# One kernel of a graph transformer: each layer gets its own numbers of sorted blocks

## The chip, the cores and the metric

The kernel runs on one core of one Trainium2 chip. The time is the device time of one execution in microseconds (us); lower is better. Engine names are those of the profile: PE (matmuls, PEld its weight loads), DVE (vector), ACT (scalar), POOL (GpSimd), SP (SyncE, which issues DMAs here).

## The reference

x is 6250 nodes x 128, and there are 200000 edges (src, dst), sorted by dst, plus one loop per node. Two layers are applied, then x + layers(x) is normalized.

```python
for l in range(2):
    xn = layernorm(x); pos = xn @ Wpos + bpos + deg_z * Wdeg + bdeg; xp = xn + pos
    q, k, v = xp @ Wq + bq, xp @ Wk + bk, xp @ Wv + bv        # 8 heads of 16
    att = clip(sum_d(q[dst] * k[src]) / 4, -50, 50)
    alpha = softmax of att over the edges of one dst
    x = x + segment_sum(v[src] * alpha, dst) @ Wo + bo
    x = x + gelu(layernorm(x) @ W1 + b1) @ W2 + b2            # 512 wide
out = layernorm(x_in + x)
```

## The kernel before

**Tables.** The nodes form NT = 49 tiles of 128. Each layer reads its keys and values from a table in HBM (kv_table[l], 256 floats a node) and its queries from q_table[l]. Set-up computes layer 0's tables; the node steps of layer 0 write layer 1's.

**Two kinds of edge units.** Since the edges are sorted by target, a tile of targets owns about 4096 of them. The first JB = 49 - 8 = 41 tiles are done *by chunks*: 1024 edges each (T = 8 tiles of 128), CPT = 4 chunks per tile of targets, CA = 4 x 41 + 1 = 165 chunks a layer. GpSimd fetches the 1024 key and value rows with eight indirect DMAs (`gather`, L1900 to L1910) into a ring of RING_KV = 4 buffers (three in kv_ring, the fourth in arena); it waits until the messages of the chunk four before are made (msg_ready). The last NB = 8 tiles are done *by blocks*: their edges have been sorted by source tile once, in layer 0, so that each source tile has 128 slots. A block part handles seven source tiles: SyncE loads their rows whole (source_rows, 896 KB, `load_sources`), and PE picks the row of each edge by a product with a one-hot matrix (`gather_rows`, L897); no indirect DMA. OB = 7 parts make a tile, UB = 56 a layer.

**A unit's work.** Both kinds go through the same steps: PE spreads the queries over the edges (L938 for chunks, L971 for blocks), DVE multiplies with the keys (L1603), reduces and clips (L1612 to L1618), ACT takes exp (L1201), DVE makes the messages (L1627, one per unit), PE sums them (L954, L987), DVE adds the sums to the accumulators (L1653, L1659, L1665). All of this is issued in an order worked out when the program is built: `unit_order` spreads the block parts evenly over the chunks from chunk FIRST_B = 17 on, the order is the same in both layers (NU = 221 units), and every unit has two slots. Into the slots go the node steps (`node_starts`, `node_steps`: 33 steps for a tile in layer 0, 27 in layer 1; projection, feed-forward, norms) and, in layer 0 only, the sorts.

**The sorts.** `sort_steps` gives each of the eight tiles 23 steps, beginning eight slots before the first part of the tile before it. A sort loads ST = 40 tiles of edges from start_tile, makes one-hots and ranks on DVE and PE (L1002, L1008, L1015), and writes the result to sorted_table, from which both layers read (`load_block`). The PSUM banks of sorts, node steps and edge sums come from one ring (`node_banks`).

**Set-up.** `count_cells` counts, for the edges from chunk COUNT_C = 163 on, how many fall into each (target tile, source tile) cell: one-hots on DVE (L1346, COUNT_STEPS = 9 steps of 32 columns, the last of 8), products on PE (L784). It shares the loop with the degree histogram (L1332, L1335, L775). `plan_chunks` checks that the graph is regular (chunk 163 starts below node 41 x 128, no cell over 128, starts at most 40 tiles apart, ...); if not, a general path runs instead.

**Places.** Semaphore targets are counted through both layers as l * NU + u (units), l * CA + c (chunks), l * UB + b (parts).

Of the kernel before, what the change touches and what calls it, by code (L numbers as in the profile page):

```python
# [72 lines left out]
NB = 8  # L73
JB = NT - NB
CA = CPT * JB + LAG
# [3 lines left out]
UB = NB * OB  # L79

FIRST_B = 17
# [19 lines left out]
def unit_order():  # L101

    order, b = [], 0
    for c in range(CA):
        order.append(("chunk", c))
        if b < UB and (c + 1 - FIRST_B) * UB >= b * (CA - 1 - FIRST_B):
            order.append(("block", b))
            b += 1
    assert b == UB
    return order  # L110


UNITS = unit_order()
NU = len(UNITS)
CHUNK_AT = [u for u, (what, _) in enumerate(UNITS) if what == "chunk"]
BLOCK_AT = [u for u, (what, _) in enumerate(UNITS) if what == "block"]
assert all(b - a > 2 for a, b in zip(BLOCK_AT, BLOCK_AT[1:]))


def is_block(u):  # L120
    return 0 <= u < NU and UNITS[u][0] == "block"


def tiles_of(u):

    return TB if is_block(u) else T


def parts_of(u):

    return 2 if is_block(u) else 1


def last_unit(j):

    return CHUNK_AT[min(CPT * (j + 1), CA - 1)] if j < JB else BLOCK_AT[(j - JB) * OB + OB - 1]

TILES = sorted(range(NT), key=lambda j: (last_unit(j), j))  # L140
POS = [TILES.index(j) for j in range(NT)]
# [20 lines left out]
def node_starts():  # L162

    starts, used = [], {}
    for i, j in enumerate(TILES):
        ready = 2 * last_unit(j) + 1
# [16 lines left out]
NODE_STARTS, NODE_USES = node_starts()  # L183


def node_steps(l):

    slots = {}
    for j, start in zip(TILES, NODE_STARTS):
# [8 lines left out]
def sort_steps():  # L198


    slots, u = {}, 0
    for s in range(NB):
        u = max(u, 2 * BLOCK_AT[(s - 1) * OB] - 8 if s else 0)
        for k in range(SORT_STEPS):
            while k in SORT_BANKED and NODE_USES.get(u, 0) >= 2:
# [5 lines left out]
        assert u + 2 <= 2 * BLOCK_AT[s * OB] - 8  # L211
    return [slots.get(u, []) for u in range(max(slots) + 1)]


SORTS = sort_steps()
# [6 lines left out]
def slots_of(l):  # L222
    return max(2 * NU + 2, len(node_steps(l)))


def unit_fills():


    fills = {-1: [("turn", u, h) for u in range(2) for h in range(parts_of(u))]}
    for u in range(NU):  # L230
        ahead = [("source", u + 3, h) for h in range(2) if is_block(u + 3)]
        turn = [("turn", u + 2, h) for h in range(parts_of(u + 2))] if u + 2 < NU else []
        hot = [("hot", u, h) for h in range(parts_of(u))]
        rows = [[("rows", u + 2, i)] if is_block(u + 2) else [] for i in range(4)]
        fills[2 * u] = turn[:1] + rows[0] + turn[1:] + rows[1] + ahead
        fills[2 * u + 1] = hot[:1] + rows[2] + hot[1:] + rows[3]
    return fills


FILLS = unit_fills()  # L240
FILL_ORDER = [f for u in range(-1, 2 * NU) for f in FILLS[u]]
# [3 lines left out]
def node_banks():  # L245

    order = []
    for l in range(L):
        for u in range(slots_of(l)):
            if u % 2 and 1 <= u // 2 <= NU:  # L250
                order.append((l, u // 2 - 1, "edges"))
            order += [(l, j, BANKED[k]) for j, k in at(node_steps(l), u) if k in BANKED]
            order += [(l, s, SORT_BANKED[k]) for s, k in (at(SORTS, u) if l == 0 else []) if k in SORT_BANKED]
# [3 lines left out]
def graph_transformer(nc, x, src, dst, Wq, bq, Wk, bk, Wv, bv, Wo, bo, Wpos, bpos, Wdeg, bdeg,  # L257
                      ln1_g, ln1_b, ln2_g, ln2_b, W1, b1, W2, b2, out):
    with ExitStack() as ctx:
# [257 lines left out]
        def nth(l, j, name):  # L517

            return (POS[j] if name in ("next_t", "qkv") else l * NT + POS[j]) + 1
# [23 lines left out]
        def ws(j):  # L543
            w = work[:, POS[j] % WORK, :]
# [9 lines left out]
        def fill(n, what, h):  # L554

            l, u = divmod(n, NU)
            return l * len(FILL_ORDER) + FILL_AT[what, u, h]

        def fills_before(l, slot):

            if slot < 0:
                return l * len(FILL_ORDER) + len(FILLS[-1]) - 1
            last = max(k for s in range(-1, slot + 1) for k in [FILL_AT[f] for f in FILLS.get(s, [])[:1 if s == slot else None]])
            return l * len(FILL_ORDER) + last

        def unit(l, u):
            return l * NU + u

        def chunk_unit(m):

            return m // CA * NU + CHUNK_AT[m % CA]

        def block_unit(m):

            return m // UB * NU + BLOCK_AT[m % UB]


        of_chunk = [not is_block(n % NU) for n in range(L * NU)]
        adds = [*itertools.accumulate(2 if chunk else 1 for chunk in of_chunk)]
        q_loads = [sum(2 if of_chunk[m] else 1 for m in range(n % 2, n + 1, 2)) for n in range(L * NU)]  # L580
# [4 lines left out]
        def hot_columns(n, h):  # L585

            if not is_block(n % NU):
                return 0, HALF_CH
            ts = part_tiles(n % NU, h)
            return ts[0] * P, len(ts) * P  # L590

        def part_tiles(u, h):
            return range(4 * h, min(4 * h + 4, tiles_of(u)))
# [58 lines left out]
        def load_plan(e, l, c):  # L652

            m = l * CA + c
# [4 lines left out]
        def load_block(e, l, b):  # L659

            m = l * UB + b
# [9 lines left out]
        def load_sources(e, l, b):  # L671
            m = l * UB + b
# [6 lines left out]
        def load_queries(e, l, u):  # L679
            n = unit(l, u)  # L680
            what, i = UNITS[u]
# [6 lines left out]
            else:  # L688
                first = (JB + i // OB) * P
                e.dma_start(q_win[:, n % 2, :], q_table[l][first:first + P, :]).then_inc(q_in[n % 2], 16)  # L690

        def sort_sync(e, s, k):
            if k == 0:
                if s >= 1:
                    e.wait_ge(sort_digit, 8 * s)
                first = e.value_load(start_tile[0:1, s:s + 1], min_val=0, max_val=START_MAX)
# [7 lines left out]
        def node_sync(e, l, j, k):  # L704
            i, n = POS[j], real(j)
# [1419 lines left out]
```

## Time and profile before

| | |
|---|---|
| median of three runs | 3759.93 us (3759.38 to 3762.02) |
| the profiled execution's own time | 3760.06 us |
| its span | 3758.3 us |
| PE busy | 2857.5 us, 76% |
| DVE busy | 2851.2 us, 76% |
| POOL busy | 2575.1 us, 69% |
| ACT busy | 1699.5 us, 45% |
| indirect gathers (L1909) | 1984 + 656 = 2640, 2524 us busy |

Busy is the time in which the engine executes an instruction; the issue of an indirect DMA adds idle time on POOL that the page puts down to "issue". The page's 40 slices show three places where POOL has little to do: the set-up (to 293 us), the turn between the layers (about 2006 to 2056 us) and the tail (from 3706 us).

### The profile page before, as it was taken

The page shows a single profiled execution, that of the slowest core. Times are in us where ns is not written, and L with a number is a line of the kernel's source. Part 1 is how long each engine was busy: PE and PEld are TensorE (multiplying, and loading weights), DVE is VectorE, ACT ScalarE, POOL GpSimd, SP SyncE. Part 2 cuts the span into 40 slices and gives each one's busy share as a digit, 9 for nine tenths or more (in the row PEclk, how much of TensorE's full clock was granted, in tenths as well). Part 3 has the DMA queues.
Part 4 walks back from the last instruction along what each step waited for, and adds up shares of the span by engine and source line. Part 5 has one row for each costly group of instructions (what it writes and reads, how often), then busy time and mean ns, then how long its engine had stood idle before and what let it go on. Part 6 is the DMA issues. An engine that isn't in the chain of part 4 may idle for free.

```text
span 3758.3 us, 71004 instructions
## 1 busy us (share of the span) xinstructions
PE 2857.5 (76%) x23719; PEld 2260.2 (60%) x23989; DVE 2851.2 (76%) x6650; ACT 1699.5 (45%) x4253; POOL 2575.1 (69%) x2665
## 2 busy tenths in 40 slices
PE   4884588788888888888886467787777887877776
PEld 3563466666666666666664345565666666656565
DVE  9886678787878888888785457677777777777775
ACT  1331236454545454545554134554555554545454
POOL 5006777776777777777773777777777777777773
PEclk6695689998989898999997679999899889999997
DMA  3015445554555555555552445555555555555552
GB/s 104 3 34 171 118 132 176 147 161 142 169 153 166 154 165 152 167 154 161 164 163 84 116 132 162 156 166 156 165 157 165 155 166 166 161 158 166 156 165 69
DMA packets 392799, 542.97 MB, mean 144 GB/s; under 512 B 77981, under 2 KB 304858, under 8 KB 392238
## 3 DMA queue, kind: packets, MB, share of 16 engines
q0 software_dynamic: 126720, 346.20, 31.6%
q1 hardware_dynamic: 258208, 184.95, 16.3%
q10 hardware_dynamic: 7506, 7.20, 0.6%
q8 instruction: 199, 3.26, 0.4%
q14 instruction: 166, 1.36, 0.1%
HBM read 512.93 MB, written 25.14 MB: 143 GB/s over the span
## 4 chain that ended last, share of the span: by engine, by line
POOL 42%; PE 21%; issue 16%; DVE 14%; ACT 4%; DMA 2%; DVEq 0%; SPq 0%; POOLq 0%; ACTq 0%
POOL kv_ring L1909 32%; POOL arena L1909 11%; PE psum L897 3%; PE psum L775 2%; PE psum L954 2%; DVE att L1612 2%; PE psum L987 2%; DVE scratch L1603 2%; PE psum L938 2%; DVE work L1315 1%; PE psum L1008 1%; PE psum L971 1%; PE psum L800 1%; DVE arena L1653 1%; DVE scratch L1627 1%
## 5 line engine op out<-in xcount | busy, mean ns | idle before, releaser
L1909 POOL DMA_INDIRECT kv_ring<-kv_table,src_idx x1984 | 1897.6, 956 | 713.6 <-issue 598.5
L1168 ACT ACTIVATE scratch<-psum 128x512 f32<-128x512 f32 x1108 | 623.5, 571 | 572.0 <-remote 239.7
L1909 POOL DMA_INDIRECT arena<-kv_table,src_idx x656 | 626.7, 955 | 202.3 <-issue 197.4
L938 PE MATMUL psum<-q_win,scratch 64*128 64x128 f32 x5280 | 447.0, 316 | 279.3 <-DVE scratch L1603 178.9
L1603 DVE TENSOR_TENSOR scratch<-psum,kv_ring 128x512 f32<-128x512 f32 x496 | 318.8, 684 | 352.7 <-DMA kv_ring<-kv_table,src_idx 323.3
L938 PEld LDWEIGHTS psum<-q_win,scratch 64*128 64x128 f32 x5280 | 379.5, 216 | 320.3 <-issue 274.2
L1612 DVE TENSOR_REDUCE att<-scratch 128x64 f32<-128x1024 f32 (+1 forms) x442 | 519.9, 1176 | 0.1
L897 PE MATMUL psum<-arena 128*128 128x256 f32 x1568 | 455.2, 416 | 58.6 <-ACT arena L1179 53.7
L954 PE MATMUL psum<-scratch 128*64 128x136 f32 x5280 | 433.6, 313 | 25.3 <-DVE work L1799 15.2
L1179 ACT COPY arena<-psum 128x512 f32<-128x512 f32 x448 | 231.4, 532 | 391.3 <-PE psum L897 380.8
L1201 ACT ACTIVATE psum<-att 128x64 f32<-128x64 f32 (+1 forms) x442 | 100.3, 227 | 640.9 <-DVE att L1618 628.9
L954 PEld LDWEIGHTS psum<-scratch 128*64 128x64 f32 x5280 | 341.5, 152 | 66.1 <-issue 40.1
L897 PEld LDWEIGHTS psum<-arena 128*128 128x128 f32 x1568 | 282.3, 200 | 163.8 <-ACT arena L1179 104.9
L1603 DVE TENSOR_TENSOR scratch<-psum,arena 128x512 f32<-128x512 f32 (+1 forms) x388 | 236.7, 646 | 168.5 <-DMA arena<-kv_table,src_idx 122.3
L1627 DVE TENSOR_TENSOR scratch<-kv_ring,psum 128x1024 f32<-128x1024 f32 x248 | 299.8, 1209 | 7.6 <-ACT psum L1201 7.3
L1653 DVE SCALAR_TENSOR_TENSOR arena<-psum,in_block,arena 128x136 f32 x660 | 204.9, 352 | 91.6 <-PE psum L954 91.2
L987 PE MATMUL psum<-scratch 128*128 128x136 f32 x1568 | 233.3, 301 | 5.1 <-ACT work L1264 3.7
L971 PE MATMUL psum<-q_win,scratch 128*128 128x128 f32 x1568 | 199.8, 280 | 38.6 <-DVE scratch L1603 20.1
L1627 DVE TENSOR_TENSOR scratch<-arena,psum 128x896 f32<-128x896 f32 (+1 forms) x194 | 219.2, 1130 | 8.9 <-ACT psum L1201 8.8
L987 PEld LDWEIGHTS psum<-scratch 128*128 128x128 f32 x1568 | 215.6, 207 | 7.8 <-issue 5.7
L971 PEld LDWEIGHTS psum<-q_win,scratch 128*128 128x128 f32 x1568 | 194.6, 196 | 22.2 <-issue 17.0
L1168 ACT ACTIVATE arena<-psum 128x512 f32<-128x512 f32 x224 | 120.0, 536 | 124.2 <-PE psum L885 65.0
(253 smaller groups left out, 4490.4 us busy)
## 6 DMA issues: line engine op xcount, KB each, us to landing
arena<-kv_table SPq DMA_DIRECT2D x112, 896.0 KB
kv_ring<-kv_table,src_idx POOLq DMA_INDIRECT x1984
q_win<-q_table SPq DMA_DIRECT2D x660, 32.0 KB
work<-kv_table SPq DMA_DIRECT2D x98, 128.0 KB
arena<-kv_table,src_idx POOLq DMA_INDIRECT x656
q_win<-q_table SPq DMA_DIRECT2D x112, 64.0 KB
work<-q_table SPq DMA_DIRECT2D x98, 64.0 KB
kv_table<-work SPq DMA_DIRECT2D x49, 128.0 KB
```

Of the source, the lines that this page charges most:

```text
L897: mm = e.matmul(to[:, t % 2 * 2 * D:(t % 2 + 1) * 2 * D], hot_source[:, t * P:(t + 1) * P], source_rows[:, t, :], start=True, stop=True)
L938: m = e.matmul(q_edge[h][:, t * P:(t + 1) * P], hotT[n % 2][h * HALF:(h + 1) * HALF, t * P:(t + 1) * P], q_win[h * HALF:(h + 1) * HALF, n ...
L954: m = e.matmul(to[h * HALF:(h + 1) * HALF], by_edge[:, t * P + h * HALF:t * P + (h + 1) * HALF], msg[n % 2][:, h * T // 2 + t, :], start=t ...
L971: m = e.matmul(q_edge[f % 2][:, (t - ts[0]) * P:(t - ts[0] + 1) * P], hotT[n % 2][:, t * P:(t + 1) * P], q_win[:, n % 2, :], start=True, s ...
L987: m = e.matmul(edge_sum(l, u), hot[n % 2][:, t, :], msg[n % 2][:, t, :], start=t == 0, stop=t == last)
L1168: e.activation(to[:, at:at + width], apart[k % 2][:, 0:width], ACT.Relu, bias=1.0, scale=-1.0).then_inc(apart_read, 1)
L1179: e.copy(kv_block[:, ts[0]:ts[-1] + 1, :].rearrange("p t d -> p (t d)"), apart[k % 2][:, 0:len(ts) * 2 * D]).then_inc(apart_read, 1)
L1603: e.tensor_tensor(prod[:, ts[0] * P:(ts[-1] + 1) * P].rearrange("p (t d) -> p t d", d=D), q_edge[f % 2][:, 0:len(ts) * P].rearrange("p (t ...
L1612: e.tensor_reduce(raw_att.rearrange("p t h -> p (t h)"), prod[:, 0:ts * P].rearrange("p (g d) -> p g d", d=HD), AX_X, ALU.add).then_inc(sc ...
L1627: e.tensor_tensor(msg[n % 2][:, 0:ts, 0:D].rearrange("p t (h d) -> p t h d", d=HD), values.rearrange("p t (h d) -> p t h d", d=HD), ex[:, ...
L1653: e.scalar_tensor_tensor(out=row, in0=of_edges, scalar=in_block[:, k, i:i + 1], in1=row, op0=ALU.mult, op1=ALU.add).then_inc(acc_added, 1)
L1909: e.indirect_dma_start(kv[m % RING_KV][:, t, :], None, kv_table[l], bass.IndirectOffsetOnAxis(ap=src_idx[:, c * T + t:c * T + t + 1], axis ...
```

## The change

Each layer gets an object of its own with its numbers and its unit order. Layer 0 keeps eight tiles by blocks from chunk 17 on. Layer 1 has ten tiles by blocks (JB = 39, 157 chunks, 70 parts) from its chunk 4 on: the eight sorted in layer 0 first, then tiles 40 and 39, which are sorted within layer 1, by the same 23 steps. The second of these sorts starts no earlier than the 22nd part. What is counted and checked in set-up covers the larger number, ten tiles. All semaphore targets follow the layers' own counts.

```diff
-NB = 8
+NBS = 8, 10
+NB = max(NBS)
 JB = NT - NB
-CA = CPT * JB + LAG
+SORTED = [*range(NT - NBS[0], NT), *range(NT - NBS[0] - 1, JB - 1, -1)]
+CA = CPT * (NT - min(NBS)) + LAG
-UB = NB * OB
-FIRST_B = 17
+FIRST_B = 17, 4
...
+class Layer:
+    def __init__(self, l, before):
+        self.nb, self.first_b = NBS[l], FIRST_B[l]
+        self.jb = NT - self.nb
+        self.ca, self.ub = CPT * self.jb + LAG, self.nb * OB
+        self.units = self.unit_order()
+        self.nu = len(self.units)
+        self.unit0, self.chunk0, self.part0 = (
+            (before.unit0 + before.nu, before.chunk0 + before.ca, before.part0 + before.ub) if before else (0, 0, 0))
...
+    def unit_order(self):
+        order, b = [], 0
+        for c in range(self.ca):
+            order.append(("chunk", c))
+            if b < self.ub and (c + 1 - self.first_b) * self.ub >= b * (self.ca - 1 - self.first_b):
+                order.append(("block", b))
+                b += 1
+    def last_unit(self, j):
+        if j < self.jb:
+            return self.chunk_at[min(CPT * (j + 1), self.ca - 1)]
+        return self.block_at[self.place(j) * OB + OB - 1]
...
-def sort_steps():
-    slots, u = {}, 0
-    for s in range(NB):
-        u = max(u, 2 * BLOCK_AT[(s - 1) * OB] - 8 if s else 0)
+def sort_steps(l):
+    slots, u, at = {}, 0, LAYERS[l].block_at
+    for s in range(NBS[0]) if l == 0 else range(NBS[0], NBS[1]):
+        if l == 0:
+            u = max(u, 2 * at[(s - 1) * OB] - 8 if s else 0)
+        else:
+            u = max(u, 2 * at[(s - NBS[0]) * 3 * OB])
...
-            m = l * CA + c
+            m = chunk(l, c)
...
-                first = (JB + i // OB) * P
+                first = SORTED[i // OB] * P
...
-                    for s, k in at(SORTS, slot) if l == 0 else []:
+                    for s, k in at(SORTS[l], slot):
...
-                e.tensor_scalar(s_dl1, s_dst, 1.0 - P * (JB + s), None, ALU.add).then_inc(sort_digit, 1)
+                e.tensor_scalar(s_dl1, s_dst, 1.0 - P * SORTED[s], None, ALU.add).then_inc(sort_digit, 1)
...
             for l in range(L):
                 wait_tables(e, l, 0)
-                for c in range(CA):
+                for c in range(LAYERS[l].ca):
                     gather(e, l, c)
```

## Rows read from the trace of the kernel before

**Rows 1.** The page, the chain that ended last.
```profile
POOL 42%; PE 21%; issue 16%; DVE 14%; ACT 4%; DMA 2%; DVEq 0%; SPq 0%; POOLq 0%; ACTq 0%
POOL kv_ring L1909 32%; POOL arena L1909 11%; PE psum L897 3%; PE psum L775 2%; PE psum L954 2%; DVE att L1612 2%; PE psum L987 2%; DVE scratch L1603 2%; PE psum L938 2%; DVE work L1315 1%; PE psum L1008 1%; PE psum L971 1%; PE psum L800 1%; DVE arena L1653 1%; DVE scratch L1627 1%
```

**Rows 2.** One line, L1909, in layer 1: ns min/median/max, first and last start; its waits.
```profile
L1909 POOL DMA_INDIRECT kv_ring<-kv_table,src_idx x992: 942/946/1052, 2056.2 to 3706.4; - x199
L1909 POOL DMA_INDIRECT arena<-kv_table,src_idx x328: 942/946/1025, 2076.2 to 3686.4; - x164
...
  DVE scratch L1627: 2.7, 9
```

**Rows 3.** One line, L1603, in layer 1: what its engine waited for (us, times).
```profile
  DMA kv_ring<-kv_table,src_idx: 258.3, 84
  DMA arena<-kv_table,src_idx: 95.7, 31
```

**Rows 4.** Busy time by stretch: from:to, length, then as its head says.
```profile
core 0: us, PE busy (x) PEld busy (x) DVE busy (x) ACT busy (x) POOL busy (x), PEclk, DMA share, GB/s
0.00:293.00 293.00, 192.78 (x2072) 149.29 (x2072) 263.02 (x439) 75.78 (x160) 50.73 (x25) 0.75 0.20 58
...
766.00:850.00 84.00, 72.30 (x613) 56.11 (x621) 71.38 (x172) 49.24 (x126) 61.84 (x66) 0.96 0.56 165
1718.00:1834.00 116.00, 101.29 (x882) 80.23 (x890) 99.72 (x238) 69.06 (x175) 85.30 (x91) 0.97 0.57 170
...
2056.00:2230.00 174.00, 89.08 (x646) 70.23 (x655) 77.64 (x151) 34.07 (x89) 131.47 (x139) 0.66 0.43 122
2230.00:3706.00 1476.00, 1140.77 (x9606) 906.64 (x9727) 1093.00 (x2646) 739.42 (x1871) 1116.77 (x1180) 0.92 0.54 160
```

**Rows 5.** L1909 in layer 0: as rows 2, and who waited for it.
```profile
L1909 POOL DMA_INDIRECT arena<-kv_table,src_idx x328: 942/946/1605, 331.5 to 1995.4; - x164
...
  DVE scratch L1627: 41.3, 17
...
  DVE scratch L1603: 91.5, 33
```

**Rows 6.** L1627 by stretch: length, DVE busy (x instructions), PEclk, DMA share, GB/s.
```profile
660.00:766.00 106.00, 13.96 (x12) 0.92 0.50 146
766.00:850.00 84.00, 15.29 (x13) 0.96 0.56 165
...
1617.00:1718.00 101.00, 12.92 (x11) 0.92 0.50 146
1718.00:1834.00 116.00, 21.08 (x18) 0.97 0.57 170
```

**Rows 7.** Groups by line and shape, 2500 to 3500 us: busy us, mean ns, idle before.
```profile
L897 PE MATMUL psum<-arena 128*128 128x256 f32 x532 | 153.3, 413 | 19.4 <-ACT arena L1179 17.6 <-ACT scratch L1168 0.9
L938 PE MATMUL psum<-q_win,scratch 64*128 64x128 f32 x1600 | 132.6, 311 | 82.4 <-DVE scratch L1603 35.9 <-DMA q_win<-q_table 28.5 <-ACT scratch L1168 15.3
L954 PE MATMUL psum<-scratch 128*64 128x136 f32 x1600 | 127.8, 307 | 6.9 <-DVE work L1799 5.8 <-DVE arena L1653 0.6 <-ACT work L1272 0.5
...
L987 PE MATMUL psum<-scratch 128*128 128x136 f32 x532 | 76.5, 293 | 0.0
...
L971 PE MATMUL psum<-q_win,scratch 128*128 128x128 f32 x546 | 69.2, 279 | 15.2 <-DVE scratch L1603 8.7 <-ACT arena L1179 5.4
```

**Rows 8.** L1627, 2056 to 2085 us: the first message multiply of layer 1.
```profile
L1627 DVE TENSOR_TENSOR scratch<-kv_ring,psum x1: 1210/1210/1210, 2079.0 to 2079.0; 128x1024 f32<-128x1024 f32 x1
```

**Rows 9.** L1909 by stretch, the two layers: POOL busy (x instructions), and the rest.
```profile
303.00:1997.00 1694.00, 1258.37 (x1312) 0.90 0.52 154
2056.00:3708.00 1652.00, 1249.32 (x1320) 0.89 0.53 156
```

**Rows 10.** L1909 in the stretch of layer 0's last sort, as rows 2.
```profile
L1909 POOL DMA_INDIRECT kv_ring<-kv_table,src_idx x53: 942/946/1571, 1627.4 to 1717.9; - x53
```

**Rows 11.** Groups by line and shape on DVE in set-up, 0 to 293 us.
```profile
L1346 DVE TENSOR_TENSOR arena<-arena,iota_rep 128x1568 bf16<-128x1568 bf16 x8 | 8.4, 1056 | 2.6 <-PE psum L784 2.6
...
L1346 DVE TENSOR_TENSOR arena<-arena,iota_rep 128x64 bf16<-128x64 bf16 x1 | 3.6, 3621 | 0.0
...
L1346 DVE TENSOR_TENSOR arena<-arena,iota_rep 128x256 bf16<-128x256 bf16 x8 | 2.3, 288 | 0.0
```

**Rows 12.** Waits of PE in layer 1: us in total, times, longest.
```profile
PE psum L938 <- DMA q_win<-q_table: 35.6, 28, 2.9
```

More of the change, by code:

```diff
@@ L98 @@
 COUNT_FIRST = 2
-def unit_order():
-    order, b = [], 0
-    for c in range(CA):
[L105 to L117, printed above, removed]
@@ L143, with layer_of @@
+LAYERS = []
+for l in range(L):
+    LAYERS.append(Layer(l, LAYERS[-1] if LAYERS else None))
+def layer_of(n):
+    l = max(l for l in range(L) if LAYERS[l].unit0 <= n)
+    return l, n - LAYERS[l].unit0
 NODE_EVERY = 10
@@ L180, in node_starts @@
     return starts, used
-NODE_STARTS, NODE_USES = node_starts()
+NODE_STARTS, NODE_USES = zip(*(node_starts(l) for l in range(L)))
 def node_steps(l):
     slots = {}
-    for j, start in zip(TILES, NODE_STARTS):
+    for j, start in zip(LAYERS[l].tiles, NODE_STARTS[l]):
         for k in range(STEPS[l]):
@@ L222, in slots_of @@
 def slots_of(l):
[L223 to L241, printed above, removed]
+    return max(2 * LAYERS[l].nu + 2, len(node_steps(l)))
+FILLS = [layer.fills() for layer in LAYERS]
+FILL_ORDER = [(l, *f) for l in range(L) for u in range(-1, 2 * LAYERS[l].nu) for f in FILLS[l][u]]
 FILL_AT = {f: k for k, f in enumerate(FILL_ORDER)}
@@ L680, in load_queries @@
             n = unit(l, u)
-            what, i = UNITS[u]
+            what, i = LAYERS[l].units[u]
             if n >= 2:
@@ L856, in plan_of @@
         def plan_of(e, n, first):
-            l, u = divmod(n, NU)
-            what, i = UNITS[u]
+            l, u = layer_of(n)
+            what, i = LAYERS[l].units[u]
             if what == "chunk":
-                m = l * CA + i
+                m = chunk(l, i)
                 if first:
@@ L1024, in node_tensor @@
             ps = node_bank(m)
-            row, col, g, qkv, own, tiny = ws(j)
+            row, col, g, qkv, own, tiny = ws(l, j)
             bank_free(e, m, held)
-            i = POS[j]
+            i = LAYERS[l].pos[j]
             done = node_mm[name]
@@ L1238, in clear_spans @@
             return [(row, min(end for end in range(row + 1, RING_W + 2) if end not in held)) for row in starts]
-        cleared_by = [sum(len(clear_spans(i)) for i in range(j)) for j in range(JB + 1)]
+        cleared_by = [[sum(len(clear_spans(i, j)) for i in range(l) for j in range(LAYERS[i].jb))
+                       + sum(len(clear_spans(l, j)) for j in range(n)) for n in range(LAYERS[l].jb + 1)] for l in range(L)]
         def node_scalar(e, l, j, k, held):
-            row, col, g, qkv, own, tiny = ws(j)
+            row, col, g, qkv, own, tiny = ws(l, j)
             i = nth(l, j, "")
@@ L1899, in gather @@
         def gather(e, l, c):
-            m = l * CA + c
+            m = chunk(l, c)
             if m >= RING_KV:
```

239 lines of the change are left out of this document (131 added, 108 removed).

## The prediction

> **What bounds the kernel now.** I began with the page: its chain gives POOL 42% of the span, nearly all of it at one line, the indirect gathers at L1909 [rows 1]. Half of a chain is not all of it, so next I cut the span into stages. 0 to 293 us is set-up, then layer 0 up to 2006 us, a turn of 50 us in which GpSimd waits for layer 1's tables, layer 1 up to 3706 us, and a tail of 52 us. The two layers do the same edge work and differ in what binds them.
>
> Layer 1: the 1320 gathers start between 2056.2 and 3706.4 us, one each 1650.2 / 1319 = 1.251 us (0.946 us of work, the rest issue). They waited only 2.7 us for a ring buffer, while the next consumer, the product at L1603, stood idle 258.3 + 95.7 = 354 us until a gather had landed [rows 2, 3]. So layer 1 runs at GpSimd's speed: 8 x 1.251 = 10.01 us a chunk, whatever the others do. From 2230 us on, where blocks are mixed in, PE is busy 77% and DVE 74% of it [rows 4].
>
> Layer 0: the ring is often full. There GpSimd waited 41.3 us for the message multiply L1627 [rows 5]. That is because of the eight sorts. I counted message multiplies (one per unit, chunk or block part) in stretches with and without a sort. Six stretches without one (766 to 850 us, 950 to 1043, 1153 to 1235, 1332 to 1420, 1527 to 1617, 1718 to 1834) hold 13 + 15 + 13 + 14 + 14 + 18 = 87 units in 553 us: 6.36 us a unit. Six with one (660 to 766, 850 to 950, 1043 to 1153, 1235 to 1332, 1420 to 1527, 1617 to 1718) hold 12 + 11 + 13 + 11 + 12 + 11 = 70 in 621 us: 8.87 us [rows 6], which shows the first and the last of each six. The product waited only 91.5 us for gathers in the whole of layer 0 [rows 5], most of it before the first block, so 6.36 and 8.87 us are the pace of PE, DVE and ACT together.
>
> **The change, part by part.** Layer 0 keeps its eight blocks, first block at chunk 17, unit order and sorts: 0 us. The turn between the layers and the tables written in it stay too.
>
> *Layer 1, gathers.* 39 tiles by chunks in place of 41 makes 4 x 39 + 1 = 157 chunks, not 165: 64 gathers fewer, 64 x 1.251 = **-80.1 us** on the engine that sets the end.
>
> *Layer 1, the others.* It gets 70 block parts in place of 56, between its chunks 4 and 156, so 153 + 70 = 223 units in 153 x 10.01 = 1531 us: GpSimd now offers 6.87 us per unit (before 148 + 56 = 204 units in 1481 us, 7.26). The engines' own pace was 6.36 us where 27% of the units were blocks; now 31% are. What a block costs PE against a chunk: its three large groups L897, L987 and L971 take 153.3/38 + 76.5/38 + 69.2/39 = 7.8 us (14 matmuls a part, so 532 are 38), a chunk's L938 and L954 (132.6 + 127.8)/100 = 2.6 us (16 a chunk) [rows 7]. So 0.04 more blocks per unit are at most 0.04 x 5.2 = 0.2 us, and on DVE nothing (a block has 7 tiles, a chunk 8). The six stretches show no slower pace where there are more blocks. I take 6.45 us, bounds 6.3 and 6.8. That is 0.42 below the 6.87, so without sorts GpSimd stays the bound.
>
> *Layer 1, two sorts.* The planner's formula puts them at units 4 to 15.5 and 71 to 83.5, 12 units each. There the pace is 8.87 + 0.1 = 8.97 us against 6.87 offered: 12 x 2.1 = 25 us of lag. The ring takes part of it: the first gather of layer 1 started at 2056.2 and its message multiply at 2079.0, 22.8 us later [rows 2, 8]; the buffer of four chunks before is then free 4 x 10.01 - 22.8 - 1.2 = 16.0 us before it is needed. Left: 25 - 16 = 9.2 us a sort. Between the sorts 55 x 0.42 = 23 us are made good, so the second finds the ring's 16 us again. **+18.4 us.** Bounds: 0 (the first falls on units with hardly any node work, and DVE is busy only 78 of the 174 us there today [rows 4]) and 2 x 25 = 50. The same arithmetic holds in layer 0: 12 x (8.87 - 7.26) = 19.3 of lag less 13 x 0.90 = 11.7 made good is 7.6 a sort; measured are 41.3 us of waits plus longer gathers, 0.959 against 0.946 us each, 16 us over 1312 [rows 9], 57 us over eight sorts: 7.2.
> In layer 0 single gathers reach 1.6 us; in the stretch of the last sort too [rows 5, 10]. The Trainium skill (SBUF — State Buffer, § Who interferes with whom) says that a VectorE copy, cast or tensor_scalar in a two-port mode locks out GpSimd, descriptor writing included, for the whole instruction; the sorts have such instructions. It speaks against the change; by it the 16 us / 8 = 2 us a sort would come on top of the ring's loss, and the sum be 4 us higher. I leave them inside, since the ring is full in the same stretch.
>
> *Set-up.* The count of cells covers 328 columns, not 264: two more full steps of L1346, 8.4/8 + 2.3/8 = 1.34 us each, and the smaller one-hot widened by a quarter, 8 x 0.07: **+3.4 us** on DVE, which is busy 263 of the first 293 us and on whose products PE's histogram waits [rows 4, 11]. Bounds 0 and 8: the last, tiny step took 3.6 us today, beside a GpSimd operation. The ten starts and flags instead of eight are some tens of ns.
>
> *SyncE.* Each block adds its row, plan and query loads; the source rows (896 KB) are 14 times more. PE already waits 35.6 us in layer 1 for query windows [rows 12]; SyncE's order puts them behind node loads. Hidden while GpSimd bounds; without that cover it is 0.2 us a unit, inside my 6.8. Tail: the planner leaves 26 half-units after the last unit, not 28: within 2 us, taken as 0.
>
> *Sum*, on the profiled execution's own 3760.1 us (span 3758.3 plus 1.8 around it; the median of the runs is 3759.9, the same): 3760.1 - 80.1 + 18.4 + 3.4 = **3702 us**.
>
> **Rivals.**
> *A, both sorts absorbed.* For it: the idle DVE where the first one falls, and layer 1's node work lacks the next layer's projection. Against: layer 0's first sorts already cost waits later. 3760.1 - 80.1 + 3.4 = 3683 us.
> *B, the engines are just too slow, 6.8 us a unit.* For it: PE is busy 86 to 87% in the stretches without sort [rows 4], and blocks are PE work. First sort 12 x (9.31 - 6.87) - 16 = 13.3; between them only 55 x 0.07 = 3.9 made good, so 25.4 for the second: 39, and 3722 us. The Trainium skill (Perfetto Trace Analysis, § Identifying the Most-Contended Engine) calls matmul busy time a bad measure of room and wants weight-load busy time; that is 67 to 69% in the same rows, so by it PE has more room and B loses weight, by matmul busy time B would be likeliest.
> *C, slower than before.* Layer 1's other engines hold a pace of 7.1 us: SyncE's in-order queue and the 14 more source loads make PE wait at each block. Then all 223 units cost the difference: 44 us at 6.87 (14 + 30), and 22.3 us for each further 0.1 us: 44 + 51 = 95 us, 3760.1 - 80.1 + 3.4 + 95 = 3778. It decides from 7.02 us a unit on. Against it: layer 0, with kv and q writes in that queue as well, ran 6.36.
> *D, it doesn't do what it says.* The checks on the graph move (chunk 155 must start below node 39 x 128). Worked out from the inputs: it starts at 4960, under 4992; the fullest cell has 109 of 128 sources, the starts lie at most 33 of 40 tiles apart. So the general path isn't taken; if it were, 62 more chunks of gathers alone would be 620 us, over 4300.
>
> **How the numbers follow.** Forecast 0.52 (own range 3692 to 3712), A 0.18, B 0.19 (3712 to 3750), C 0.10 with its approach to no change, D 0.01. Range: from A, 3681, into most of B, 3742; above it lies some 0.12, below 0.04. 0.2%, 7.5 us, is about what can be told from no change. The forecast, A and most of B are faster: 0.88; same 0.03; slower 0.09.
>
> **What would show it.** 1256 gathers in layer 1, 1.25 us apart, from about 2060 to 3646 us. Two groups of ring waits on L1627, 8 to 12 us each, near 2160 and 2660 us; more, spread over layer 1, would say B or C, none A. L1346 with 10 full steps, and the first gather 3 us later. Units without a sort would show the product still waiting for gathers in layer 1, far less than 354 us. Wrong is the forecast if gathers of layer 1 wait over 35 us for the ring, or if single gathers grow.

## The result, and the profile after

The changed kernel takes **3699.43 us** (median of 4 runs, 3693.64 to 3701.53), the kernel before on the same chip 3759.65 us (4 runs, 3757.09 to 3762.02): ratio 0.984, 95% interval 0.9826 to 0.9854. 3702 us was predicted. The profiled execution took 3699.51 us; its span is 3697.7 us, 60.6 us less than before. From the page of the changed kernel, busy time and the chain that ended last:

```profile
PE 2986.3 (81%) x24671; PEld 2336.4 (63%) x24671; DVE 2910.8 (79%) x6776; ACT 1763.5 (48%) x4391; POOL 2521.1 (68%) x2601
...
PE 43%; DVE 21%; ACT 11%; POOL 10%; issue 8%; DMA 5%; SPq 1%; DVEq 1%; ACTq 0%; POOLq 0%
PE psum L937 9%; POOL kv_ring L1951 7%; PE psum L1027 5%; PE psum L994 4%; PE psum L978 4%; DVE att L1655 4%; DMA arena<-sorted_table 3%; DVE work L1358 3%; PE psum L1011 2%; POOL arena L1951 2%; DVE scratch L1646 2%; PE psum L955 2%; ACT arena L1219 2%; PE psum L815 2%; ACT scratch L1208 2%
```

POOL has fallen from 42% to 10% of the chain [rows 1], and PE seems to be the bound. The lines say something else. The gathers (L1951, was L1909) of layer 1 [rows 2], and the product (L1646, was L1603) that consumes them [rows 3]; ns min/median/max, first and last start, then what the engine waited for in us and times:

```profile
L1951 POOL DMA_INDIRECT kv_ring<-kv_table,src_idx x944: 941/947/1421, 2053.9 to 3643.7; - x189
L1951 POOL DMA_INDIRECT arena<-kv_table,src_idx x312: 942/947/1474, 2073.9 to 3623.7; - x156
...
  DVE scratch L1670: 20.8, 19
```
```profile
L1646 DVE TENSOR_TENSOR scratch<-psum,kv_ring x236: 676/681/693, 2065.8 to 3649.0; 128x512 f32<-128x512 f32 x118
...
  DMA kv_ring<-kv_table,src_idx: 53.0, 18
  PE psum L978: 23.1, 21
  DMA arena<-kv_table,src_idx: 18.6, 6
```

1256 gathers fill 2053.9 to 3643.7 us: 1589.8 us, of which 1255 x 1.251 = 1570.1 us are GpSimd's own pace. So it is held back only 19.7 us in the whole layer. But the product waits for gathers only 53.0 + 18.6 = 71.6 us, not 354. The two sides are now close. The chain from 2770 us to the last gather, a stretch in which no gather waited for the ring, begins:

```profile
by line: PE psum L937 12.7%; PE psum L1027 7.9%; DMA arena<-sorted_table 7.2%; issue 5.9%; PE psum L994 5.0%; DVE att L1655 4.4%; PE psum L978 4.0%; ACT scratch L1208 3.4%; PE psum L955 3.2%; PE psum L1011 3.1%; ACT L1318 2.8%; ACT arena L1
```

In the kernel before, gathers are 64.7% of it from 2770 us to the last gather, and issue 21.7%. So in the changed kernel a second path, through PE, DVE, ACT and the blocks' loads from the sorted table, reaches the end of the layer unbroken and about as late as the gathers, and a chain names only one of two paths of nearly equal length. Layer 0, whose order of units did not change, shows how little decides which one: gathers are 26.0% of the chain there in the trace of before and 17.7% in that of after.

Where the 60.6 us of span went, stretch by stretch, after less before:

| stretch | before, us | after, us | difference |
|---|---|---|---|
| start to first gather | 293.2 | 291.4 | -1.8 |
| layer 0, first to last gather | 1712.2 | 1709.9 | -2.3 |
| turn | 50.8 | 52.6 | +1.8 |
| layer 1, first to last gather | 1650.2 | 1589.8 | -60.4 |
| last gather to end | 51.9 | 54.0 | +2.1 |

Everything lies in layer 1. There the message multiply (L1670, was L1627), one per unit, cut at the starts of the two sorts and their ends (length, DVE busy and starts, PEclk, DMA share, GB/s; an instruction that starts at a bound is counted on both sides):

```profile
2107.00:2207.00 100.00, 13.96 (x12) 0.85 0.51 149
2207.00:2580.00 373.00, 64.19 (x56) 0.95 0.58 171
2580.00:2690.00 110.00, 15.14 (x13) 0.89 0.51 149
2690.00:3022.00 332.00, 58.33 (x50) 0.94 0.57 168
3022.00:3654.00 632.00, 107.21 (x92) 0.93 0.56 167
```

By the exact starts (2107.0, 2207.6, 2580.0, 2690.6, 3022.6 us) the pace is 8.38 us a unit in the first sort (12 units), 6.77 between them (55), 8.51 in the second (13), and 6.64 behind it (50; the first 20 of these took 6.86, the other 30 6.49). Two views say what set the 6.77. The product between the sorts, 2207 to 2580 us, has no wait for a gather:

```profile
  PE psum L978: 7.2, 6
  PE psum L1011: 0.4, 1
  issue: 0.2, 1
```

and the engines there are as follows (PE, PEld, DVE, ACT, POOL busy, PEclk, DMA share, GB/s; the second row is a late stretch, where the product waits for gathers again):

```profile
2207.00:2580.00 373.00, 314.24 (x2670) 246.26 (x2667) 294.11 (x708) 207.16 (x521) 282.19 (x298) 0.95 0.58 171
3022.00:3643.00 621.00, 521.55 (x4371) 411.65 (x4369) 482.62 (x1168) 340.95 (x858) 469.86 (x497) 0.93 0.57 169
```

So 6.77 us was the other engines' own pace, with PE 84% busy (PEld 66%), hardly under the 6.87 that GpSimd offers. What GpSimd waited for the message multiply, 2060 to 2630, 2630 to 2800 and 2800 to 3690 us (us, times, longest):

```profile
POOL kv_ring L1951 <- DVE scratch L1670: 1.5, 5, 0.3
POOL arena L1951 <- DVE scratch L1670: 0.3, 1, 0.3
```
```profile
POOL kv_ring L1951 <- DVE scratch L1670: 12.6, 5, 3.7
POOL arena L1951 <- DVE scratch L1670: 4.6, 2, 4.0
```
```profile
POOL kv_ring L1951 <- DVE scratch L1670: 1.2, 4, 0.3
POOL arena L1951 <- DVE scratch L1670: 0.6, 2, 0.3
```

Waits of 0.3 us are ordinary issue time that ended on this semaphore. Real ones exist in one place only, at the *second* sort: 17.2 us in 7, about 15 beyond issue. Two of them (2641 and 2676 us) lie in the sort and hold GpSimd 7.2 us beyond issue; four (2697 to 2764 us) lie in the 75 us behind it and hold it 7.7. The first sort cost no wait.

The lead of a gather over its message multiply shows why. It was 22.8 us at the start of layer 1 (2053.9 to 2076.7). At 2101.1 us, just before the first sort, the message is that of chunk 3, whose gathers began at 2083.9: 17.2 us. At 2207.6 us it is chunk 12, gathered from 2175.3: 32.3 us. The other engines had fallen back by 16.3 us; the lead grew by 15.1, since the gathers themselves were 1.2 us late by then. At 2573.8 us, chunk 49, gathered from 2546.2: 27.6 us. The second sort sets the other engines back by 22.2 us (chunks 49 to 59 took 2573.8 to 2696.0 us, not 100.1), and the ring had 4 x 10.01 - 1.2 - 27.6 = 11.2 us left: 11 us remain for the sort, and GpSimd meets a part of them only behind it. The other 4 of the 15 come from the units there: the ring was full, and the first ten took 7.17 us each, more than the 6.87 offered.

Single gathers grew too, and the longest lie in the two sorts: up to 1259 ns in the first, 1474 in the second, at most 1058 elsewhere. The longest of all, and what ran on DVE beside it:

```profile
2648.62 1.47 POOL L1951 DMA_INDIRECT arena<-kv_table,src_idx  x1 [0.31 <-issue]
2648.47 0.82 DVE L1749 TENSOR_TENSOR arena<-arena,iota_rep 128x1280 bf16<-128x1280 bf16 x1
2649.20 0.73 DVE L1752 TENSOR_TENSOR arena<-arena 128x490 bf16<-128x490 bf16 x2
```

The sorts' tensor_tensor instructions with both inputs in SBUF (L1729, L1749, L1752, L1771) are where it happens: the 28 gathers of layer 1 that overlap one of them take 1074 ns on average, which is 3.6 us of the growth. The 13 that overlap only a tensor_scalar or a cast of the sorts take 946. The gathers of layer 1 (from:to, length, POOL busy, PEclk, DMA share, GB/s), where before 1320 took 1249.32 us [rows 9]:

```profile
2054.00:3645.00 1591.00, 1193.04 (x1256) 0.92 0.56 166
```

0.950 us each against 0.9465, 4.3 us over the layer. Waits of 15 and growth of 4.3 give the 19.7 us.

Last, two waits of PE in layer 1, and the set-up. Query windows cost less than before (27.8 us, 35.6 before [rows 12]); a block's load of its plan from the sorted table costs 50.0 us, where the same group had 20.7 us before from 2230 us on. The full steps of L1389 (was L1346 [rows 11]):

```profile
PE psum L925 <- DMA arena<-sorted_table: 50.0, 35, 3.3
...
PE psum L978 <- DMA q_win<-q_table: 27.8, 22, 1.7
```
```profile
L1389 DVE TENSOR_TENSOR arena<-arena,iota_rep 128x1568 bf16<-128x1568 bf16 x10 | 10.6, 1064 | 1.2 <-PE psum L824 1.2
L1389 DVE TENSOR_TENSOR arena<-arena,iota_rep 128x320 bf16<-128x320 bf16 x10 | 3.1, 312 | 0.0
```

Ten full steps take 10.6 + 3.1 us as worked out, but the last small step, 128x80 now, takes 0.2 us where its like (128x64) took 3.6 before. The first gather came at 291.4 us instead of 293.2. In the other executions below it came between 285.7 and 298.0 us, so a term of 3 us can't be told there.

### The profile page after: what moved, and what is told of

The parts are those of the page before. It is cut to its first block, busy times and chain, and to the rows that moved or that the text cites. A ratio compares the mean times of both kernels' runs of the same rounds, so it can differ in the third digit from the quotient of the medians.

```text
span 3697.7 us, 72970 instructions
## 1 busy us (share of the span) xinstructions
PE 2986.3 (81%) x24671; PEld 2336.4 (63%) x24671; DVE 2910.8 (79%) x6776; ACT 1763.5 (48%) x4391; POOL 2521.1 (68%) x2601
## 4 chain that ended last, share of the span: by engine, by line
PE 43%; DVE 21%; ACT 11%; POOL 10%; issue 8%; DMA 5%; SPq 1%; DVEq 1%; ACTq 0%; POOLq 0%
PE psum L937 9%; POOL kv_ring L1951 7%; PE psum L1027 5%; PE psum L994 4%; PE psum L978 4%; DVE att L1655 4%; DMA arena<-sorted_table 3%; DVE work L1358 3%; PE psum L1011 2%; POOL arena L1951 2%; DVE scratch L1646 2%; PE psum L955 2%; ACT arena L1219 2%; PE psum L815 2%; ACT scratch L1208 2%
## 5 line engine op out<-in xcount | busy, mean ns | idle before, releaser
L1951 POOL DMA_INDIRECT kv_ring<-kv_table,src_idx x1936 | 1854.8, 958 | 709.0 <-issue 580.4
L1208 ACT ACTIVATE scratch<-psum 128x512 f32<-128x512 f32 x1148 | 646.7, 570 | 596.7 <-PE psum L947 374.3
L1951 POOL DMA_INDIRECT arena<-kv_table,src_idx x640 | 612.7, 957 | 202.8 <-issue 192.6
L937 PE MATMUL psum<-arena 128*128 128x256 f32 x1764 | 505.4, 409 | 64.6 <-ACT arena L1219 60.8
L978 PE MATMUL psum<-q_win,scratch 64*128 64x128 f32 x5152 | 419.0, 308 | 98.4 <-DVE scratch L1646 61.5
L978 PEld LDWEIGHTS psum<-q_win,scratch 64*128 64x128 f32 x5152 | 353.9, 208 | 209.4 <-issue 165.2
L1219 ACT COPY arena<-psum 128x512 f32<-128x512 f32 x504 | 263.4, 532 | 443.6 <-PE psum L937 434.5
L1646 DVE TENSOR_TENSOR scratch<-psum,kv_ring 128x512 f32<-128x512 f32 x484 | 310.5, 683 | 156.0 <-DMA kv_ring<-kv_table,src_idx 116.8
L937 PEld LDWEIGHTS psum<-arena 128*128 128x128 f32 x1764 | 311.1, 197 | 170.7 <-ACT arena L1219 117.1
L1646 DVE TENSOR_TENSOR scratch<-psum,arena 128x512 f32<-128x512 f32 (+1 forms) x412 | 250.4, 643 | 92.4 <-DMA arena<-kv_table,src_idx 42.1
L1670 DVE TENSOR_TENSOR scratch<-kv_ring,psum 128x1024 f32<-128x1024 f32 x242 | 292.4, 1208 | 19.7 <-ACT psum L1241 19.1
L1027 PE MATMUL psum<-scratch 128*128 128x136 f32 x1764 | 265.5, 299 | 7.0 <-ACT work L1307 4.4
L1027 PEld LDWEIGHTS psum<-scratch 128*128 128x128 f32 x1764 | 245.4, 205 | 12.1 <-issue 8.0
L1670 DVE TENSOR_TENSOR scratch<-arena,psum 128x896 f32<-128x896 f32 (+1 forms) x206 | 231.9, 1126 | 13.7 <-ACT psum L1241 13.4
L1011 PEld LDWEIGHTS psum<-q_win,scratch 128*128 128x128 f32 x1764 | 220.1, 196 | 11.5 <-issue 3.4
```

Of the source, the lines that this page charges most:

```text
L937: mm = e.matmul(to[:, t % 2 * 2 * D:(t % 2 + 1) * 2 * D], hot_source[:, t * P:(t + 1) * P], source_rows[:, t, :], start=True, stop=True)
L978: m = e.matmul(q_edge[h][:, t * P:(t + 1) * P], hotT[n % 2][h * HALF:(h + 1) * HALF, t * P:(t + 1) * P], q_win[h * HALF:(h + 1) * HALF, n ...
L1011: m = e.matmul(q_edge[f % 2][:, (t - ts[0]) * P:(t - ts[0] + 1) * P], hotT[n % 2][:, t * P:(t + 1) * P], q_win[:, n % 2, :], start=True, s ...
L1027: m = e.matmul(edge_sum(l, u), hot[n % 2][:, t, :], msg[n % 2][:, t, :], start=t == 0, stop=t == last)
L1208: e.activation(to[:, at:at + width], apart[k % 2][:, 0:width], ACT.Relu, bias=1.0, scale=-1.0).then_inc(apart_read, 1)
L1219: e.copy(kv_block[:, ts[0]:ts[-1] + 1, :].rearrange("p t d -> p (t d)"), apart[k % 2][:, 0:len(ts) * 2 * D]).then_inc(apart_read, 1)
```

## The experiments

### One plain DMA in place of eight gathers

Theory (forecast): without GpSimd's limit the other engines would run layer 1 at about 6.45 us a unit. Rival B: 6.8. The gather's eight indirect DMAs become one of the same 1 MB, which reads consecutive rows.

```
-            for t in range(T):
-                e.indirect_dma_start(kv[m % RING_KV][:, t, :], None, kv_table[l], ...).then_inc(gathered[m % RING_KV], 16)
+            first = c % (NT - T) * P
+            e.dma_start(kv[m % RING_KV], kv_table[l][first:first + CH, :].rearrange("(t p) d -> p t d", p=P)
+                        ).then_inc(gathered[m % RING_KV], 16)
```

In p_before this is made in the kernel before, in p_after in the changed one. p_after_early also loads a block's plan (its slots, from sorted_table; not its source rows) one unit earlier, and p_after_nosort leaves out the two sorts of layer 1 (tiles 40 and 39 take the plans of two tiles sorted in layer 0):

```
+                for u in range(5):                        # p_after_early
+                    if LAYERS[l].is_block(u):
+                        load_block(e, l, LAYERS[l].units[u][1])
...
-                        if LAYERS[l].is_block(u + 4):
-                            load_block(e, l, LAYERS[l].units[u + 4][1])
+                        if LAYERS[l].is_block(u + 5):
+                            load_block(e, l, LAYERS[l].units[u + 5][1])
-SORTS = [sort_steps(l) for l in range(L)]                 # p_after_nosort
+SORTS = [sort_steps(0), []]
...
+            s = s - NBS[0] if s >= NBS[0] else s
```

> The kernel before, with each chunk's eight indirect gathers replaced by one plain load of 1024 rows of the same size (other rows, so the attention of the chunk edges is left out of what is computed rightly). GpSimd then no longer sets any pace, and layer 1's message multiplies (221 units, first to last) show what PE, DVE and ACT can do by themselves where 27% of the units are blocks and no sort runs. Theory F (my forecast: 6.36 us a unit): 220 x 6.36 = 1400 us in layer 1. Theory T (layer 1 has a slower own pace than layer 0, since SyncE's in-order queue and late small loads hold PE): 6.6 us or more, 1450 us or more.

> The changed kernel with the same replacement of the gathers. 227 units in layer 1, 24 of them beside a sort. Theory F (6.45 us a unit, 8.97 beside a sort): 202 x 6.45 + 24 x 8.97 = 1518 us in layer 1. Theory B (blocks cost PE so much that the pace is 6.8 us): 202 x 6.8 + 24 x 9.3 = 1597 us. Theory T (the plan loads of the blocks come late, PE waited 50 us for them in layer 1 of the changed kernel's trace): as B in time, but with the waits of L925 for sorted_table still there and near 50 us.

> p_after, and each block's plan (the load from sorted_table) issued one unit earlier. Theory T: the 50 us of PE's waits for that load go and layer 1 gets 30 to 50 us shorter than in p_after. Theory B: the waits go but PE is as busy as it was, layer 1 within 10 us of p_after.

> p_after without the two sorts in layer 1 (tiles 40 and 39 read the plans of tiles 41 and 42, so their sums are left wrong). All theories: the difference to p_after is what two sorts cost the engines. Forecast: 24 x 2.5 = 60 us. If the sorts of layer 1 are cheaper than those of layer 0 (the first one sank into the ring without a wait in the changed kernel's trace): 35 to 45 us. Divided by 227, layer 1 then shows the pace without sorts: F 6.45, B and T 6.8.

One execution each, the kernel before beside them 3752.69 us: p_before 3537.74, p_after 3721.93, p_after_early 3679.15, p_after_nosort 3669.92 us. The message multiply in layer 1, in this order (ns, first and last start):

```profile
L1627 DVE TENSOR_TENSOR scratch<-kv_ring,psum x124: 1186/1212/1223, 2030.7 to 3492.0; 128x1024 f32<-128x1024 f32 x124
```
```profile
L1670 DVE TENSOR_TENSOR scratch<-kv_ring,psum x118: 1184/1212/1223, 2040.7 to 3676.6; 128x1024 f32<-128x1024 f32 x118
```
```profile
L1673 DVE TENSOR_TENSOR scratch<-kv_ring,psum x118: 1186/1214/1223, 2031.7 to 3635.4; 128x1024 f32<-128x1024 f32 x118
```
```profile
L1671 DVE TENSOR_TENSOR scratch<-kv_ring,psum x118: 1184/1214/1223, 2038.0 to 3624.7; 128x1024 f32<-128x1024 f32 x118
```

| kernel | first to last message | units between | us a unit |
|---|---|---|---|
| p_before | 1461.3 | 220 | 6.64 |
| p_after | 1635.9 | 226 | 7.24 |
| p_after_early | 1603.7 | 226 | 7.10 |
| p_after_nosort | 1586.7 | 226 | 7.02 |

Both kernels are slower in layer 1 than the forecast's theory had them (1461 us against 1400, 1636 against 1518), and p_after is slower than rival B's 1597 too. It is even *slower* than the changed kernel itself (3699), so the plain DMA isn't a neutral stand-in. PE's waits for tables are one thing that changed, p_before and then p_after:

```profile
PE psum L938 <- DMA q_win<-q_table: 100.8, 64, 4.4
PE psum L885 <- DMA arena<-sorted_table: 26.8, 22, 2.3
```
```profile
PE psum L978 <- DMA q_win<-q_table: 89.2, 50, 4.0
PE psum L925 <- DMA arena<-sorted_table: 45.1, 33, 3.9
```

The 32 KB query windows are waited for 89 to 113 us in the four, where the kernels with gathers have 28 to 55. These paces are therefore taken as upper bounds; only differences between the four are used, and each is of two single executions. The early loads give 32.2 us. With and without the sorts layer 1 differs by 1635.9 - 1586.7 = 49.2 us, 24.6 a sort, but only part of it lies beside the sorts. In the first sort's 12 units the two kernels take 95.8 and 78.4 us, in the second's 13 they take 115.4 and 96.8: 1.45 and 1.43 us more a unit, 17.4 and 18.6 us a sort. The second stretch is slow even without its sort, 7.44 us a unit.

p_after_nosort is 0.38 us a unit slower than p_before over the whole layer, but p_before begins with 16 intervals of chunks alone, at 5.70 us each. From the 17th unit on, where 31% and 27% of the units are blocks, it is 7.07 against 6.72 us: 0.35 more, where 0.09 was taken. PE's waits for the blocks' plans are 56.0 us against 26.8, 0.13 of it; the rest, 0.22, is about the upper bound of 0.2 that rows 7 gave.

### Gathers cut to six, early loads, no sorts

six_before and six_after leave out two of each chunk's eight gathers (`range(T if m < RING_KV else T - 2)`, with the product's wait to match), in the kernel before and in the changed one. early_plan is the changed kernel with the early loads alone, no_sort1 the changed kernel without the two sorts.

> The kernel before with six of each chunk's eight gathers (two tiles of 128 edges keep the rows of an earlier chunk, so that part of the sums is left wrong): GpSimd needs 7.5 us a chunk and sets no pace, while its transfers stay as spread out as in the full kernel, which the plain loads of the first four runs were not (PE waited over 100 us for query windows behind them). Layer 1, first to last message: 1400 us if the engines' own pace is my 6.36 us a unit; 1450 to 1460 if it is the 6.64 of the plain loads.

> The changed kernel with six of eight gathers. Layer 1, 226 intervals: 1518 us by my forecast (6.45 without, 8.97 with a sort); 1560 to 1597 if the pace without sorts is 6.6 to 6.8 because blocks are dearer or their loads late. The full kernel took 1577.5 us with GpSimd needing 1570.

> The changed kernel, complete, with each block's plan loaded one unit earlier. If late plan loads took the room that the ring waits show (50 us of PE's waits in layer 1): those waits fall below 10 us, the 15.2 us of GpSimd's ring waits in layer 1 nearly vanish, and the kernel is 8 to 15 us faster than the changed one, 3685 to 3692 us. If PE's block work took it: no difference beyond 3 us.

> The changed kernel without the two sorts in layer 1 (tiles 40 and 39 read the plans of tiles 41 and 42, their sums are left wrong). By the ring account the 15.2 us of ring waits and the 3.7 us of longer gathers in layer 1 are the sorts', so 17 to 19 us less: 3680 to 3683 us, gathers of layer 1 within 1 us of 1255 x 1.251 = 1570. If the pace without sorts is at or over 6.87 us a unit, part of the ring waits stays and the gain is under 12 us.

They came out at 4838.81, 4788.19, 5642.9 and 5605.01 us. The kernel before on that chip had a median of 5697.7 us (11 runs, 5681 to 5727), half as long again as elsewhere. The last two were run once more on another chip:

> The kernel of early_plan again: its runs fell on a chip on which the kernel before took 5698 us, with waits of 10 to 30 us for semaphores everywhere, which says nothing about this question. If late plan loads took the room that the ring waits show: PE's 50 us of waits for them in layer 1 fall below 10, the 15.2 us of ring waits there nearly vanish, ratio to the kernel before 0.980 to 0.982 (3685 to 3692 us) against 0.984 of the changed kernel. If PE's block work took it: 0.984, no difference beyond 0.001.

> The kernel of no_sort1 again, for the same reason (no sorts in layer 1; tiles 40 and 39 read the plans of tiles 41 and 42, their sums are left wrong). Ring account: ring waits and longer gathers of layer 1 (15.2 + 3.7 us) go, gathers of layer 1 take 1570 us, 3680 to 3683 us, ratio 0.979. If the pace without sorts is itself at 6.87 us a unit or over: part of the ring waits stays, ratio 0.981 to 0.983.

There too the kernel before took 5693.45 us (11 runs), early_plan2 5624.99 and no_sort1b 5599.17 us. The longest waits of early_plan2 (us, times, longest):

```profile
POOL kv_ring L1954 <- DVE scratch L1673: 1566.3, 202, 18.9
ACT scratch L1211 <- remote: 1527.2, 309, 23.2
DVE arena L1699 <- remote: 1218.6, 143, 19.0
```

The ring is nearly always full, and ACT and DVE stand still for up to 23 us at a time until something ends that the profile puts outside the core's engines. That is another bottleneck than the one in question, so these six runs say nothing of the change at 3.7 ms: all their changed kernels are faster than the kernel before there (early loads 0.989 [0.9852, 0.9928] and 0.9896 [0.986, 0.9931]; without sorts 0.9821 [0.9789, 0.9853] and 0.9855 [0.9811, 0.9899]), for reasons that weren't looked into. What made these executions long stays open.

### Early loads alone

The same edit as in p_after_early, on the changed kernel with its gathers, on a chip on which the kernel before takes its usual time.

> The kernel of early_plan a third time: both calls before fell on chips on which the kernel before takes 5.7 ms, with PE standing still for 6 to 20 us at a time. On a chip on which the kernel before takes 3.76 ms: if late plan loads took the room that the ring waits show, PE's 50 us of waits for them in layer 1 fall below 10, the 15.2 us of ring waits there nearly vanish, ratio 0.980 to 0.982 (3685 to 3692 us) against the changed kernel's 0.984. If PE's block work took it: 0.984, no difference beyond 0.001.

**3687.41 us** (5 runs, 3677.51 to 3706.69) against 3755.58 us of the kernel before there (9 runs): ratio 0.9805 [0.9786, 0.9825], where the change alone has 0.984 [0.9826, 0.9854]. The intervals just miss each other, so it is probably some 12 us faster than the changed kernel, and it is faster than the kernel before. The two were not run side by side. The profile is that of its slowest run (span 3704.9 us). In it PE's waits for sorted rows are gone from the list (those for query windows rose from 27.8 to 38.2 us), and the product (here L1649) has room again, 152.7 us of waits for gathers against 71.6:

```profile
  DMA kv_ring<-kv_table,src_idx: 117.2, 44
  DMA arena<-kv_table,src_idx: 35.5, 13
```
```profile
2118.00:2219.00 101.00, 13.99 (x12) 0.85 0.51 148
2219.00:2596.00 377.00, 64.14 (x55) 0.92 0.57 171
2596.00:2707.00 111.00, 15.16 (x13) 0.89 0.49 144
2707.00:3031.00 324.00, 58.24 (x50) 0.98 0.58 173
```

These are message multiplies in the same stretches as above. Behind the second sort 50 units take 324.4 us, 6.49 each against 6.64, but between the sorts 55 take 376.9, 6.85 against 6.77, there too with no wait for a gather. TensorE's granted clock goes the same way, 0.98 against 0.94 behind the second sort and 0.92 against 0.95 between the two, so one execution each doesn't tell what the late loads took of the engines' pace. The sorts are as before (101.3 / 12 = 8.44 and 110.7 / 13 = 8.51), and so is what the ring lost:

```profile
L1954 POOL DMA_INDIRECT kv_ring<-kv_table,src_idx x944: 942/946/1951, 2065.2 to 3653.8; - x189
...
  DVE scratch L1673: 18.2, 11
```

1588.6 us for the 1256 gathers, 1.2 us less than the changed kernel. So the median came out in the range given beforehand, but not for the reason given: the ring waits were to vanish nearly, and they did not. The lead before the second sort was 33.3 us here, the sort set the others back by 21.9, and 21.9 - (38.8 - 33.3) = 16 us were to remain; some 14 were measured. That execution's first gather came at 298.0 us. Where the 12 us of the median come from is not in this profile. What did change is the chain, from 2770 us to the last gather:

```profile
by line: POOL kv_ring L1954 52.4%; issue 23.2%; POOL arena L1954 18.7%; DVE scratch L1673 0.8%; DMA arena<-kv_table,src_idx 0.6%; DVE scratch L1649 0.6%; PE psum L940 0.4%; DMA kv_ring<-kv_table,src_idx 0.3%; DMA q_win<-q_table 0.3%; DVE at
```

It runs through the gathers again, as in the kernel before. By this one execution, the second path of the changed kernel hung on the late loads.

### Set-up and first block alone

The changed kernel's code with eight blocks in layer 1, but with their first at chunk 4 and the set-up of ten tiles. This undoes the 64 gathers and two sorts and keeps the rest.

```
-NBS = 8, 10
-NB = max(NBS)
+NBS = 8, 8
+NB = 10
...
-            e.wait_ge(sort_out, 16 * NB)
+            e.wait_ge(sort_out, 16 * max(NBS))
```

> The change without its two added tiles: set-up counts and checks ten tiles, blocks of layer 1 begin at its chunk 4, but both layers keep eight tiles by blocks, so layer 1 keeps its 1320 gathers and has no sort. What is left is what the change does beside the 64 gathers and the sorts. By my sum: +3.4 us for set-up and 0 for the early start, since GpSimd sets layer 1's pace anyway: 3763 us, ratio 1.001. By the changed kernel's trace, whose first gather came 1.8 us earlier and not later: 3756 to 3760, ratio 0.999 to 1.000. If the early start of the blocks itself brought part of the gain: 3740 or less.

3756.99 us (12 runs) against 3757.46 us (17 runs): ratio 1.0005 [0.9994, 1.0017]. No change, and its layer 1 has the pace of before to a tenth of a us, 3703.1 - 2052.9 = 1650.2 us:

```profile
L1951 POOL DMA_INDIRECT kv_ring<-kv_table,src_idx x992: 942/946/1076, 2052.9 to 3703.1; - x199
...
  DVE scratch L1670: 3.0, 10
```

By the interval, set-up, tables and the earlier blocks are together worth between 3757 x 0.0006 = 2.3 us gained and 3757 x 0.0017 = 6.4 us lost; the gain hangs on the two tiles taken from the gathers.

## Why the prediction was right, step by step

- **What bounds.** Right. GpSimd bound layer 1: setup_first leaves it its 1320 gathers and gets the same 1650.2 us.
- **64 gathers, -80.1 us.** Right: 1256 remain, 1.251 us apart outside the sorts and the ring waits. With the sorts' +18.4 layer 1 was to lose 61.7 us; it lost 60.4.
- **Two sorts, +18.4 us.** The sum is right (19.7), its steps are not: two errors cancelled. *First*, the step "between the sorts 55 x 0.42 = 23 us are made good, so the second finds the ring's 16 us again" failed. The own pace there was 6.77, not 6.45, and the lead went only from 32.3 to 27.6 us. *Second*, the "12 x 2.1 = 25 us of lag" of the first sort was 16.3 us, inside the ring. So it is not 9.2 + 9.2 but 0 + 15, and 4.3 us of longer gathers. The premium of a sort over its surroundings was 8.38 - 6.77 = 1.6 us a unit, and 1.45 and 1.43 by the plain kernels, where 2.5 had been carried over from layer 0 [rows 6]. And some 4 of the 15 us are not the second sort's but those of slow units behind it. That the sum came out near is luck.
- **6.45 us a unit, bounds 6.3 and 6.8.** Mis-sized: 6.77, at the upper bound. The plain kernels put 0.22 on the blocks' share, where 0.09 was taken, and PE waited 50.0 us for the blocks' plans, 29 us more than before, or 0.13 us a unit: 6.36 + 0.22 + 0.13 = 6.71. That is near, but not shown: with the loads early the pace between the sorts was 6.85. A rival that no run separates is TensorE's clock, which the sum left out: it was granted at 0.96 to 1.00 in the six stretches that gave 6.36, and at 0.95 between the sorts, where a matmul of L978 took 304 ns against 285 at 1.00 (L938 before, 1332 to 1420 us). SyncE's term had been put on the query windows, which got better; it was the other load of the same queue.
- **The rule of longer gathers** (SBUF — State Buffer, § Who interferes with whom, in the Trainium skill). By it a copy, cast or tensor_scalar in a two-port mode holds up the writing of GpSimd's descriptors. The size fits, 2 us a sort worked out and 4.3 us for two measured, but the cause does not: gathers beside the sorts' tensor_scalar and cast instructions kept their 946 ns, and those that grew ran beside tensor_tensor instructions, 1074 ns on average. Leaving it outside the sum did no harm only because the ring's part came out smaller.
- **Set-up, +3.4 us.** Not to be told: first gathers of all executions lie 12 us apart. The two larger steps came as worked out; the last small one took 0.2 us instead of 3.6.
- **Rivals.** A was half true: the first sort was absorbed, the second not. B had the pace and missed the price: at 6.8 it made the first sort cost 13.3 us and the second 25.4, because both used the premium of layer 0. With what the sorts cost in fact, 15 + 4.3 us, B's sum is 3683 + 19 = 3702 us, the forecast's own: the time doesn't tell the two apart, the stretches do, and they speak for B's pace. The rule of the Trainium skill (Perfetto Trace Analysis, § Identifying the Most-Contended Engine) to read room from weight-load time rather than matmul time took weight from B; here it was 66% against 84%, and the other engines were nevertheless at their own pace, with no wait for a gather. In this trace neither share measured the room that was left. C needs over 7.02 us a unit; p_after_nosort stands exactly there and p_after over it, but only with the 1 MB bursts. D didn't happen.
- **Signs to look for.** 1256 gathers up to 3644 us, named as 3646: right. Two groups of ring waits: one, at 2641 to 2765 us. Product still waiting for gathers, far less than 354 us: 71.6, but none of it between the sorts. First gather 3 us later: 1.8 earlier. And one sign that was to show the forecast wrong did come, in small: single gathers grew, by 4.3 us in all.

The prediction also says of layer 0 that most of the product's 91.5 us of waits for gathers came before the first block; up to there (495 us) they were 54.0, somewhat over half.

What stays open: why a sort costs 1.4 to 1.6 us a unit in layer 1 and 2.5 in layer 0; the place of the first one (little node work beside it) isn't the reason, since the two premiums are the same. The changed kernel without its two sorts has no run at 3.7 ms, and ten blocks from chunk 17 on, or nine blocks, weren't tried.

## What to carry to other kernels

When work is taken from the engine that sets the pace, work out how far the next engine's own pace lies below it; here that was 0.42 us a unit on paper and 0.10 in fact, and the gain held, as far as the runs show, because only two short disturbances had to be made up. A disturbance costs what it sets the consumers back less what is left of the ring, and what is left must be followed from one to the next: read the lead of producer over consumer at each, rather than take it as restored. When two paths are nearly equally long, a chain of waits shows one of them and can swing to the other between two kernels, or between two executions of the same code; ask the producer's own line how much of its span it was held.

## What was not expected of the hardware

- Eight gathers of 128 KB, one 1.251 us after the other, go with shorter waits for small loads than one plain DMA of 1 MB: PE's waits for 32 KB query windows in layer 1 were 28 to 55 us with gathers and 89 to 113 us with plain DMAs, and the changed kernel without any indirect gather (3721.93 us) was slower than with them (3699.43). The plain DMAs also come as soon as the ring is free, with nothing to space them; which of the two it is was not tried.
- The kernel before took 3748 to 3765 us in four groups of runs, but 5681 to 5727 us in a fifth and 5656 to 5716 in a sixth. In the long executions engines stand still for up to 23 us at a time; TensorE's granted clock was 0.72 to 0.74 there, 0.87 to 0.88 otherwise. One of the two chips later ran it in the usual time.
- A DVE instruction over 128x64 elements took 3.6 us beside a GpSimd operation in set-up [rows 11]; its like over 128x80 in the changed kernel, at 61 us and also beside a GpSimd operation (34.1 to 65.0 us), took 0.2 us.
- GpSimd's indirect gathers, 0.946 us each, grow to 1.07 us on average, and up to 1.47, beside tensor_tensor instructions of DVE with both inputs in SBUF, and not beside its tensor_scalar and cast instructions.
